# Twelve fused layers on one core: set-up steps of five stages reordered, and a small first key load

## The chip, the core and the metric

The kernel runs on one core of a Trainium2 chip. The engines are TensorE (PE, with its weight loads as PEld), VectorE (DVE), ScalarE (ACT), GpSimd (POOL) and SyncE (SP), which here only issues loads. The metric is device time in microseconds (us) of one execution, lower is better: the median of three runs of the kernel before is 1064.81 us (1062.67 to 1066.28).

## The reference

A latent `x` of 64 rows by 256 passes through four blocks of cross-attention, self-attention and feed-forward, each added to `x` after a normalisation. The context has 6272 rows of 256. Only what the change touches is shown.

```python
x = x + _L0_attn_ref(_layernorm(x), ...)      # stage 1: 16 heads, causal
x = x + _L0_ffn_ref(_layernorm(x), ...)       # stage 2: shared SiLU gate/up/down, and routed experts, top 2 of 8
x = x + _L1_xattn_ref(_layernorm(x), ctx_2048, ...)   # stage 3: queries, keys and values rounded to 8-bit steps
x = x + _L1_ffn_ref(...)                      # stage 5: LoRA experts, top 2 of 8
x = x + _L2_xattn_ref(...)                    # stage 6
#   ln_out = _ln(hidden_states, ln_w, ln_b)
#   q, k, v, qx = four fp8-rounded linear layers of ln_out; q, k, qx normalised per head of 128
#   kx, vx = split(cond @ w_kv_x); kx normalised per head
#   core = attention(q, k, v); xout = attention(qx, kx, vx)
#   out = fp8(concat(core, xout) / proj_smooth) @ wproj
x = x + _L3_attn_ref(...)                     # stage 10: short and long convolution
x = x + _L3_ffn_ref(...)                      # stage 11: 2 shared and 16 routed experts with biases b1, b2, top 4
```

## The kernel before, in words

Stages 0 to 11 follow each other, since each needs `x`. Ahead of them a sweep over the context (L1480, L1491, L1514) makes the keys and values of stages 0 and 3. Every engine has its own instruction stream, written out by hand; semaphores join them. So the order of the code within a stage is the order on the engine, and an instruction that waits holds up all that stand behind it there. Between two stages there is a serial chain: `x` gets its residual (L599), two statistics instructions (L537, L538), the variance (L548), a power on GpSimd (L562), the normalised `xn` (L542), a transpose on PE (L577), its copy on ACT (L582).

`busy(pe, n, b)` (L528) issues n products of constants that nobody reads; they only fill TensorE's time.

Weights come in pieces of up to 2048 columns (1 MB) into a ring of four slots. SP's loop (L2936) waits until `weights_used` says that a slot's old piece was used, then issues the load. The piece `x2_kx` (keys of the context in stage 6, for all eight groups of heads) is the first of stage 6 and keeps its slot through the stage; the others rotate through the other three slots.

- **Stages 0 to 2 and the rounding of the values.** Stage 3 needs the 49 tiles of values as integers. DVE makes them in nine parts of up to six tiles (`quantise`, L1706, into one of two buffers), ACT narrows each part (`narrow_values`, L1714). Part p waits until part p - 2 was narrowed. The parts are spread over stages 0, 1 and 2: in stage 1 parts 3 and 4 stand ahead of the attention and part 5 behind it; in stage 2 parts 6, 7 and 8 (the last is one tile) stand between the normalisation and the activation L892. ACT narrows them after the small tanh L925.
- **Stage 2, `f0_tensor`.** Gate and up products (L827), routed part (L868, L872), filler (6), transposes of the hidden rows (L879, L881), down product (L834), routed output (L886). DVE ranks the router's logits (L905 to L914) after the activation.
- **Stage 3, `x1_vector`.** DVE adds the bias q1 (L1934), multiplies by 0.25 (L1935), finds a step per head, rounds to `x1_q_rows` (L1940, 64x1024), PE transposes all eight pairs (L1859), DVE masks them (L1947, 128x1024), and only then the first scores (L1874) start.
- **Stages 5 and 6.** At the end of stage 5 DVE scales the low-rank rows (L1053), then waits for the whole piece `x2_kx` and centres the keys' weights of group 0 (`x2_key_weights`, L2090, L2092, L2094), and only then adds the residual (L599, L1060). PE's first products of stage 6 (L2109, keys of group 0) need those weights. Six blocks of projections follow (L2132: qx0, qx1, q0, q1, k, v), with head normalisation on DVE (`moments_of` L2354 to L2360, `normalise` L2370) and ACT (L2629), transposes on PE (`turn`, L2144), their copies on ACT (L2636), a constant product (L2150), and then the loop over groups: `variance` (L2188, L2189), `scores` (L2205), DVE's scaling (L2420).
- **Stages 10 and 11.** Stage 10 has fillers of three between its spectrum product (L1225), the inverse transform (L1234) and the output product (L1240). Stage 11 starts on PE with nine products that place the bias b1 of the expert pairs (L1327), then three fillers, then the transposes of `xn` (L577), the logits (L1331) and the experts (L1340).

## Time and profile before

| | |
|---|---|
| median of three runs | 1064.81 us (1062.67 to 1066.28) |
| profiled execution, its own time | 1061.59 us |
| its span | 1059.8 us |
| busy: PE, PEld, DVE, ACT, POOL | 994.1, 657.2, 716.2, 358.4, 156.9 us |
| share of the chain that ended last: PE, DVE, issue, DMA, ACT, POOL | 73%, 11%, 5%, 4%, 3%, 3% |
| mean granted clock of TensorE | 0.99 |

The span covers all but 1.8 us of the profiled execution. The time is 94% PE, but that is an average: from about 250 to 300 us and from 386 to 450 us, and again behind 930 us, small stages pass `x` from engine to engine, and the chain runs over DVE, ACT, POOL and loads as much as over PE.

### The profile page before, as it was taken

Reading aid. Unit: us, or ns where it says so; the run is one execution under the profiler, and the core shown is the slowest. Engines: PE = TensorE matmul, PEld = TensorE weight load, DVE = VectorE, ACT = ScalarE, POOL = GpSimd, SP = SyncE. Lnnn points to the kernel's source line nnn. Section 1 sums busy time; section 2 is a strip of 40 time slices with the busy share of each in tenths; the row PEclk is TensorE's granted clock in tenths of the full one; section 3 lists DMA queues with packets and bytes.
Section 4 is the critical chain, followed back from the end, with each engine's and each line's share of the span. In section 5 each row is a group of like instructions: output and inputs, shape, how many; then the busy total and the mean of one; then the engine's idle time right before and its main releaser. Section 6 shows DMA issues by size and latency. Waiting matters only on the chain.

```text
span 1059.8 us, 20606 instructions
## 1 busy us (share of the span) xinstructions
PE 994.1 (94%) x7822; PEld 657.2 (62%) x7846; DVE 716.2 (68%) x1909; ACT 358.4 (34%) x627; POOL 156.9 (15%) x143
## 2 busy tenths in 40 slices
PE   6999999998789988899999999999999999988898
PEld 4776677675335544365777777677777777743455
DVE  3777767768779834787676767767676767743343
ACT  2332333334428721443333333333343332301211
POOL 0000000001000010233222323222222323000000
PEclk9999999999999999998999999999999999899999
DMA  7100101002229996860000000000000000232430
GB/s 284 41 22 22 38 20 40 20 5 96 99 62 188 192 313 217 320 241 2 1 1 1 1 0 0 0 0 0 0 0 0 0 1 2 79 140 88 174 159 4
DMA packets 68729, 76.09 MB, mean 72 GB/s; under 512 B 52544, under 2 KB 59456, under 8 KB 64832
## 3 DMA queue, kind: packets, MB, share of 16 engines
q1 hardware_dynamic: 68240, 74.71, 23.1%
q8 instruction: 36, 0.59, 0.2%
q10 hardware_dynamic: 432, 0.62, 0.2%
q14 instruction: 21, 0.17, 0.0%
HBM read 62.41 MB, written 0.07 MB: 59 GB/s over the span
## 4 chain that ended last, share of the span: by engine, by line
PE 73%; DVE 11%; issue 5%; DMA 4%; ACT 3%; POOL 3%; SPq 0%; DVEq 0%; POOLq 0%; PEldq 0%
PE ps L2215 15%; PE ps L2109 13%; PE ps L1480 8%; PE ps L2205 7%; PE ps L1470 4%; PE ps L1491 4%; PE ps L1514 2%; PE ps L1526 2%; POOL x_sum L2733 2%; ACT vals L2016 2%; DMA x_keys<-vals 2%; DVE S L2420 1%; PE ps L528 1%; PE ps L1874 1%; PE ps L2817 1%
## 5 line engine op out<-in xcount | busy, mean ns | idle before, releaser
L2215 PE MATMUL ps<-vals,S 128*128 128x257 f32 x784 | 188.5, 384 | 0.7 <-ACT S L2665 0.7
L2109 PE MATMUL ps<-keysT,row_biases_sb 128*128 128x512 f32 (+1 forms) x416 | 186.3, 573 | 1.0 <-DVE row_biases_sb L2094 0.9
L2733 POOL TENSOR_TENSOR x_sum<-x_max,consts 128x4 f32<-128x4 f32 (+1 forms) x104 | 133.6, 1285 | 322.4 <-DVE x_max L2408 322.4
L2420 DVE SCALAR_TENSOR_TENSOR S<-ps,x_sum,keysT 128x128 f32<-128x128 f32 x392 | 110.9, 344 | 73.3 <-PE ps L2215 64.2
L2215 PEld LDWEIGHTS ps<-vals,S 128*128 128x128 f32 x784 | 143.3, 192 | 19.0 <-issue 1.0
L2665 ACT ACTIVATE S<-S 128x512 f32<-128x512 f32 (+1 forms) x104 | 62.7, 606 | 219.1 <-DVE S L2455 218.5
L2205 PE MATMUL ps<-x_q,x_keys 128*128 128x128 f32 x784 | 114.2, 288 | 0.0
L2109 PEld LDWEIGHTS ps<-keysT,row_biases_sb 128*128 128x128 f32 x416 | 76.6, 192 | 57.7 <-issue 52.6
L2205 PEld LDWEIGHTS ps<-x_q,x_keys 128*128 128x128 f32 x784 | 96.4, 193 | 0.0
L1480 PE MATMUL ps<-ring,S 128*128 128x512 f32 x196 | 92.2, 593 | 0.5 <-DVE ps L1621 0.5
L2597 ACT COPY x_keys<-ps 128x512 f32<-128x512 f32 (+1 forms) x104 | 57.1, 549 | 67.5 <-PE ps L2109 34.3
L1594 ACT ACTIVATE S<-ps 128x2048 f32<-128x2048 f32 (+1 forms) x25 | 46.1, 1843 | 82.3 <-PE ps L1526 76.1
L528 PE MATMUL ps<-consts 128*128 128x512 bf16 x253 | 65.7, 380 | 3.7 <-issue 0.5
L2397 DVE TENSOR_TENSOR sw_key_out<-wide 128x512 bf16<-128x512 f32 (+1 forms) x104 | 67.7, 652 | 0.7 <-ACT wide L2604 0.7
L2455 DVE TENSOR_TENSOR S<-S,xnT 128x512 f32<-128x512 f32 (+1 forms) x104 | 66.7, 654 | 0.3
L2432 DVE TENSOR_TENSOR wide<-wide,S 128x512 f32<-128x512 f32 x96 | 63.3, 659 | 0.3
L2604 ACT ACTIVATE wide<-ps 128x512 f32<-128x512 f32 (+1 forms) x104 | 60.0, 577 | 0.0
L1642 DVE TENSOR_SCALAR S<-ps,mask_sb 128x256 f32<-128x256 f32 x49 | 23.7, 484 | 52.6 <-PE ps L1480 31.1
L1470 PE MATMUL ps<-S,ring 128*128 128x256 f32 (+1 forms) x200 | 50.8, 398 | 8.9 <-DMA S<-ctxT 8.2
L1480 PEld LDWEIGHTS ps<-ring,S 128*128 128x128 f32 x196 | 35.3, 190 | 25.9 <-issue 24.7
L562 POOL TENSOR_TENSOR rstd<-var_eps,consts 64x1 f32<-64x1 f32 x13 | 7.1, 550 | 296.4 <-DVE var_eps L548 260.0
L2408 DVE TENSOR_SCALAR x_max<-ps 128x4 f32<-128x4 f32 (+1 forms) x104 | 16.5, 159 | 48.4 <-PE ps L2189 48.3
(453 smaller groups left out, 1366.1 us busy)
## 6 DMA issues: line engine op xcount, KB each, us to landing
ring<-weights SPq DMA_DIRECT2D x24, 1024.0 KB, 5.9
keysT<-ctxT SPq DMA_DIRECT2D x2, 3136.0 KB, 14.9
vals<-ctxN SPq DMA_DIRECT2D x1, 6272.0 KB, 24.3
S<-ctxT SPq DMA_DIRECT2D x12, 512.0 KB, 4.1
ring<-weights SPq DMA_DIRECT2D x6, 768.0 KB, 7.1
keysT<-weights SPq DMA_DIRECT2D x1, 1792.0 KB, 8.8
keysT<-weights SPq DMA_DIRECT2D x1, 1536.0 KB, 12.0
row_biases_sb<-row_biases SPq DMA_DIRECT2D x1, 1416.0 KB, 12.0
```

What stands on the lines that cost most here:

```text
L528: pe.matmul(ps[:, b, :], product[:, 0:128], moving, start=True, stop=True)
L1470: ins = pe.matmul(ps[:, sw_keys_bank, TWO * o:TWO * o + n * TILE], w[:, 256 * k + 128 * o:256 * k + 128 * o + 128], sw_ctxT[ph][:, k, TWO ...
L1480: ins = pe.matmul(bank(sw_vk_bank), sw_ctxT[ph][:, k, a:a + TILE], w[:, 512 + 768 * k:1024 + 768 * k], start=k == 0, stop=k == KT - 1)
L2109: ins = pe.matmul(ps[:, x2_key_bank(g, c), 0:width(c)], x2_wk[:, k, :], ctxT[:, k, span(c)], start=k == 0, stop=k == KT - 1)
L2205: ins = pe.matmul(ps[:, 3 + c % 2, 128 * s:128 * s + 128], x2_keys[:, c % 2, TILE * s:TILE * s + TILE], x2_q[:, :], start=True, stop=True)
L2215: ins = pe.matmul(bank(6, D + 1), S[:, a:a + TILE], ctx_and_ones[:, SUB * c + s, :], start=c == 0 and s == 0, stop=c == NC - 1 and s == su ...
L2397: dve.tensor_tensor(x2_low[c % 2][:, 0:width(c)], x2_dev[:, c % 2, 0:width(c)], high_half(c), ALU.subtract)\
L2420: ins = dve.scalar_tensor_tensor(S[:, a:a + TILE], ps[:, 3 + c % 2, 128 * s:128 * s + 128], x2_inv[:, c % 2, s:s + 1], x2_tile_const, ALU. ...
L2432: ins = dve.tensor_tensor(best, best, S[:, span(c)], ALU.max)
L2455: dve.tensor_tensor(chunk, chunk, spread(x2_top, 1, subs(c)), ALU.subtract).then_inc(sem("x2_shifted"), 1)
L2665: act.activation(chunk, chunk, ACT.Exp, scale=SCALE2).then_inc(sem("x2_exp"), 1)
L2733: pool.tensor_tensor(x2_inv[:, c % 2, 0:n], x2_var[:, c % 2, 0:n], C("neg_half").broadcast_to([128, n]), ALU.pow)\
```

## The change

It has seven parts. (1) Stage 1: one part of the rounding less ahead of the attention (3, then 4 behind it). (2) Stage 2: parts 5, 6 and the one-tile part (now number 7) ahead of the activation, the last six tiles (number 8) behind the router's ranking; ACT narrows in another order; the six fillers become two, and two more stand before the down product. POOL scales the bias q1 by 0.25 in this stage. (3) Stage 3: add and multiply are one instruction; rounding, transposes and mask go in two halves, the scores start after the first, and six fillers become three. (4) The 128 columns of `x2_kx` that group 0 needs are loaded by themselves, behind the last experts of stage 5, into `x2_wk`, and DVE centres them before it scales the low-rank rows. (5) The piece `x2_kx` is loaded sixth to seventh instead of first, and the pieces k, v, kx, vx are released by the end of blocks 0 to 3. (6) Stage 6: `turn(3)` before the third keys' product, the two `low_half` before the wait for the constants, ACT's `normalise(2)` one place earlier. (7) Of the nine bias products of stage 11 three each take the place of three fillers in stage 10; three remain, with four fillers behind them.

```diff
-    + [(6, "x2_kx", 2048), (6, "x2_qx0", 2048), (6, "x2_qx1", 2048), (6, "x2_q0", 2048), (6, "x2_q1", 2048), (6, "x2_k", 2048),
-       (6, "x2_v", 2048), (6, "x2_vx", 2048)]
+    + [(6, "x2_qx0", 2048), (6, "x2_qx1", 2048), (6, "x2_q0", 2048), (6, "x2_q1", 2048), (6, "x2_k", 2048),
+       (6, "x2_v", 2048), (6, "x2_kx", 2048), (6, "x2_vx", 2048)]
...
-                     10: (4, 1), 11: (3, 5)}
+                     10: (4, 1), 11: (4, 5)}
...
                 if s == 1:
-                    quantise(dve, 3, 4)
+                    quantise(dve, 3)
                 mha_vector(dve, s)
                 if s == 1:
-                    quantise(dve, 5)
+                    quantise(dve, 4)
...
-            busy(pe, 6, 6)
+            busy(pe, 2, 6)
             pe.wait_ge(sem("f0_hidden"), since("f0_hidden", 1))
...
+            busy(pe, 2, 4)
             pe.wait_ge(sem("f0_hT"), since("f0_hT", 1))
...
             norm_vector(dve, 2)
-            quantise(dve, 6, 7, 8)
+            quantise(dve, 5, 6, 7)
...
             link(dve, "dve", dve.tensor_reduce(f0_weight, f0_exp, AX, ALU.add))
+            quantise(dve, 8)
...
             norm_scalar(act, 2)
+            narrow_values(act, 5)
             act.wait_ge(sem("f0_part_psum"), 1)
             act.activation(f0_act, bank(0), ACT.Tanh, scale=0.5).then_inc(sem("f0_tanh"), 1)
+            narrow_values(act, 6)
...
-            narrow_values(act, 6, 7, 8)
...
+            narrow_values(act, 7, 8)
...
+                pool.tensor_scalar(R("q1"), R("q1"), 0.25, None, ALU.mult)
...
+            if runs(6):
+                dve.wait_ge(sem("x2_first_in"), 16)
+                x2_key_weights(dve, 0)
             dve.wait_ge(sem("f1_lows_psum"), since("f1_lows_psum", 1))
...
-            if runs(6):
-                weights_here(dve, "x2_kx")
-                x2_key_weights(dve, 0)
...
-            busy(pe, 3, 7)
+            f3_biases(pe, F3_BIASES[0])
             pe.wait_ge(sem("a3_left_ready"), since("a3_left_ready", 1))
...
-            busy(pe, 3, 7)
+            f3_biases(pe, F3_BIASES[1])
             pe.wait_ge(sem("a3_y_ready"), since("a3_y_ready", 1))
...
+        F3_BIASES = ((0, 1, 4), (2, 3, 5), (6, 7, 8))
...
+        value_parts = [(6 * i, 6 * i + 6) for i in range(7)] + [(48, NT), (42, 48)]
...
-            busy(pe, 6, 3)
+            for i in range(2):
+                pe.wait_ge(sem("x1_q_ready"), since("x1_q_ready", i + 1))
+                for j in range(4):
+                    a = 512 * i + 128 * j
+                    ins = pe.transpose(ps[:, X1_TURNED[i], j * T:(j + 1) * T], x1_q_rows[:, a:a + 128], C("ident")[0:T, 0:T])
+                ins.then_inc(sem("x1_qT_psum"), 1)
+            busy(pe, 3, 3)
...
-            link(dve, "dve", dve.tensor_tensor(x1_q, bank(0, D, T), R("q1"), ALU.add))
-            link(dve, "dve", dve.tensor_scalar(x1_q, x1_q, 0.25, None, ALU.mult))
+            link(dve, "dve", dve.scalar_tensor_tensor(x1_q, bank(0, D, T), 0.25, R("q1"), ALU.mult, ALU.add))
...
+            x1_tile_of(dve, 0)
...
+            x1_tile_of(dve, 1)
...
+        x2_behind_block = {"x2_k": 0, "x2_v": 1, "x2_kx": 2, "x2_vx": 3} if runs(5) and runs(6) else {}
...
+            turn(3)
             keys(0, 2)
-            turn(3)
...
+            low_half(0, 0)
+            low_half(0, 1)
             dve.wait_ge(sem("x2_const_ready"), since("x2_const_ready", 2))
             tile(0)
-            low_half(0, 0)
-            low_half(0, 1)
             read_var(0, 0)
+            weights_here(dve, "x2_kx")
...
             take_heads(0)
+            normalise(2)
             take_heads(1)
-            normalise(2)
...
+                if name == "f1_experts3" and runs(6):
+                    first = piece_from["x2_kx"]
+                    sp.dma_start(x2_wk, cut(io["weights"][:, first:first + KT * 1024], KT, 1024)[:, :, 0:GD]).then_inc(sem("x2_first_in"), 16)
...
-                sp.wait_ge(weights_used, release_before[n])
+                if pieces[n][1] in x2_behind_block:
+                    sp.wait_ge(sem("x2_block_psum"), x2_behind_block[pieces[n][1]] + 1)
+                else:
+                    sp.wait_ge(weights_used, n - NSLOT + 1)
                 load(n)
```

The order of the instructions at three places follows. On DVE in stage 2, from the ranking's last steps to the normalisation, first before, then now (`wide<-vals,S` is a part of the rounding, `x_sb` is `x`).

```order
L910 TENSOR_TENSOR S<-S 64x8 [waits logits_exp,dve_step]
L911 TENSOR_REDUCE S<-S 64x1 [waits dve_step]
L914 TENSOR_REDUCE S<-S 64x1 [waits dve_step]
L917 TENSOR_TENSOR x_sb<-x_sb,ps 64x256 [waits out_psum,dve_step]
L918 SCALAR_TENSOR_TENSOR x_sb<-ps,S,x_sb 64x256 [waits dve_step]
```

```order
L896 TENSOR_TENSOR S<-S 64x8 [waits logits_exp,dve_step]
L897 TENSOR_REDUCE S<-S 64x1 [waits dve_step]
L900 TENSOR_REDUCE S<-S 64x1 [waits dve_step]
L1711 TENSOR_TENSOR wide<-vals,S 128x1536 [waits values_narrowed,dve_step]
L904 TENSOR_TENSOR x_sb<-x_sb,ps 64x256 [waits out_psum]
L905 SCALAR_TENSOR_TENSOR x_sb<-ps,S,x_sb 64x256 [waits dve_step]
```

One part of the rounding moved from stage 1 to ahead of the activation, and one now stands between the ranking and the residual. On DVE at the end of stage 5, first before, then now (`x_small` holds the means of the keys' weights, `row_biases_sb` holds the centred weights):

```order
L1050 SCALAR_TENSOR_TENSOR S<-S,ps 128x128 [waits dve_step]
L1053 TENSOR_SCALAR S<-ps 64x4x16 [waits low_psum]
L2090 TENSOR_REDUCE x_small<-ring 128x2 [waits weights_in0]
L2092 TENSOR_SCALAR x_small<-x_small 128x2 [waits x2_wk_sum]
L2094 TENSOR_TENSOR row_biases_sb<-ring,x_small 128x256 [waits x2_wk_sum]
L599 TENSOR_TENSOR x_sb<-x_sb,ps 64x256 [waits out_psum]
```

```order
L1044 SCALAR_TENSOR_TENSOR S<-S,ps 128x128 [waits dve_step]
L2107 TENSOR_REDUCE x_small<-row_biases_sb 128x2 [waits x2_first_in]
L2109 TENSOR_SCALAR x_small<-x_small 128x2 [waits x2_wk_sum]
L2111 TENSOR_TENSOR row_biases_sb<-row_biases_sb,x_small 128x256 [waits x2_wk_sum]
L1050 TENSOR_SCALAR S<-ps 64x4x16 [waits low_psum]
L584 TENSOR_TENSOR x_sb<-x_sb,ps 64x256 [waits out_psum]
```

The three weight steps moved ahead of the low-rank rows and wait for the small load in place of the ring's. On PE from stage 10's spectrum product to stage 11's transposes, first before, then now (`ring,S 128x176` are the bias products, `consts 128x512` the fillers):

```order
L1225 MATMUL ps<-S,consts 65x256 [waits once_copied]
L528 MATMUL ps<-consts 128x512 x3
L1234 MATMUL ps<-consts,S 128x64 [waits once_ready]
L1240 MATMUL ps<-ring,S 64x256 [waits once_ready]
L1327 MATMUL ps<-ring,S 128x176 [waits out_psum,gates_tanh,weights_in2]
L1327 MATMUL ps<-ring,S 128x176 x8
L577 MATMUL ps<-consts,xn 128x64 [waits norm_ready]
```

```order
L1219 MATMUL ps<-S,consts 65x256 [waits once_copied]
L1324 MATMUL ps<-ring,S 128x176 [waits gates_tanh,weights_in0]
L1324 MATMUL ps<-ring,S 128x176 x2
L1228 MATMUL ps<-consts,S 128x64 [waits once_ready]
L1234 MATMUL ps<-ring,S 64x256 [waits once_ready]
L1324 MATMUL ps<-ring,S 128x176 [waits out_psum,gates_tanh,weights_in0]
L513 MATMUL ps<-consts 128x512 x4
L562 MATMUL ps<-consts,xn 128x64 [waits norm_ready]
```

Six of the nine products now stand in stage 10 (the second three, ahead of L1234, are not repeated), three where all nine stood.

## Rows read from the trace of the kernel before

**Rows 1.** Timeline, stage 1: start us, us, engine, line, what, [idle before <-releaser].
```profile
263.85 3.96 DVE L1706 TENSOR_TENSOR wide<-vals,S 128x1536 int16<-128x1536 f32 x2
...
264.65 1.94 PE L673 MATMUL ps<-ring,xnT 128*64 128x512 f32 x8 [0.45 <-ACT xnT L582]
...
267.73 0.68 DVE L727 TENSOR_TENSOR S<-ps,row_biases_sb 128x512 f32<-128x512 f32 x1
```

**Rows 2.** Timeline, stage 2.
```profile
280.67 3.43 DVE L1706 TENSOR_TENSOR wide<-vals,S 128x1536 int16<-128x1536 f32 x2
...
281.38 3.65 PE L827 MATMUL ps<-ring,xnT 128*64 128x512 f32 x16 [0.35 <-ACT xnT L582]
...
286.11 3.14 ACT L1714 CAST vals<-wide 128x1536 f16<-128x1536 int16 x3
...
287.95 0.68 DVE L892 SCALAR_TENSOR_TENSOR S<-S,ps 128x512 f32<-128x512 f32 x1
...
289.78 0.15 DVE L905 COPY S<-ps 64x8 f32<-64x8 f32 x1
...
292.56 0.15 DVE L914 TENSOR_REDUCE S<-S 64x1 f32<-64x8 f32 x1
...
293.42 0.87 DVE L917 TENSOR_TENSOR x_sb<-x_sb,ps 64x256 f32<-64x256 f32 x2 [0.70 <-PE ps L886]
```

**Rows 3.** Timeline, stage 1: a GpSimd addition beside DVE's rounding.
```profile
264.15 2.04 POOL L592 TENSOR_TENSOR x_sb<-x_sb,row_biases_sb 64x256 f32<-64x256 f32 x1
```

**Rows 4.** Timeline, stage 3 until the first scores.
```profile
300.77 0.68 DVE L1940 TENSOR_SCALAR S<-sw_key_out 64x1024 f32<-64x1024 f32 x1
...
302.15 1.47 PE L528 MATMUL ps<-consts 128*128 128x512 bf16 x6
302.33 1.22 DVE L1947 TENSOR_TENSOR x_probsT<-ps,consts 128x1024 f32<-128x1024 f32 x1 [0.38 <-PE ps L1859]
...
303.61 1.99 PE L1874 MATMUL ps<-keysT,x_probsT 32*128 32x512 f32 x12
```

**Rows 5.** Timeline, end of stage 5.
```profile
419.98 0.46 DVE L1053 TENSOR_SCALAR S<-ps 64x64 f32<-64x64 f32 x2 [3.08 <-PE ps L995]
...
421.07 0.65 PE L1019 MATMUL ps<-wide,S 128*64 128x256 f32 x2 [0.30 <-ACT S L1084]
421.41 0.42 DVE L2090 TENSOR_REDUCE x_small<-ring 128x2 f32<-128x256 f32 x1 [0.97 <-DMA ring<-weights]
...
422.52 0.41 DVE L599 TENSOR_TENSOR x_sb<-x_sb,ps 64x256 f32<-64x256 f32 x1
```

**Rows 6.** Chain of waits, set-up of stage 6: start us, us, what.
```profile
433.10 5.88 DMA ring<-weights
```

**Rows 7.** Timeline, set-up of stage 6.
```profile
428.56 5.37 PE L2132 MATMUL ps<-ring,S 128*64 128x512 f32 x24 [0.93 <-DVE S L2344]
...
449.34 0.16 DVE L2408 TENSOR_SCALAR x_max<-ps 128x4 f32<-128x4 f32 x1 [1.07 <-PE ps L2189]
```

**Rows 8.** DVE's waits, 431.28 to 449.34: total us, times, longest.
```profile
DVE S L2354 <- PE ps L2132: 1.9, 2, 1.0
...
DVE S L2370 <- POOL S L2738: 0.9, 1, 0.9
```

**Rows 9.** Timeline, stages 10 and 11.
```profile
1036.78 2.92 PE L1327 MATMUL ps<-ring,S 128*128 128x176 f32 x18 [0.30 <-PE ps L1240]
...
1038.43 0.41 DVE L542 TENSOR_SCALAR xn<-x_sb,moments,rstd 64x256 f32<-64x256 f32 x1 [0.66 <-POOL rstd L562]
...
1040.29 0.33 PE L577 MATMUL ps<-consts,xn 64*128 64x64 f32 x2
```

**Rows 10.** Timeline, keys' products at the first and second group change.
```profile
486.58 5.48 PE L2109 MATMUL ps<-keysT,row_biases_sb 128*128 128x512 f32 x8
...
546.64 3.60 PE L2109 MATMUL ps<-keysT,row_biases_sb 128*128 128x512 f32 x8
```

**Rows 11.** Stretch: us, busy us of PE, PEld, DVE, ACT, POOL; clock, DMA share, GB/s.
```profile
482.00:490.00 8.00, 6.56 (x24) 4.07 (x25) 6.98 (x21) 0.24 (x2) 3.81 (x3) 0.59 0.01 2
```

More of the change, by code:

```diff
@@ L931, in f0_scalar, with f0_pool @@
             act.activation(f0_exp, f0_exp, ACT.Exp).then_inc(sem("f0_router_exp"), 1)
-        STAGES[2] = (f0_tensor, f0_vector, f0_scalar, lambda pool: norm_pool(pool, 2))
+            narrow_values(act, 7, 8)
+        def f0_pool(pool):
+            norm_pool(pool, 2)
+            if runs(3):
+                pool.tensor_scalar(R("q1"), R("q1"), 0.25, None, ALU.mult)
+        STAGES[2] = (f0_tensor, f0_vector, f0_scalar, f0_pool)
         f1_low_weights = wide[:, :, :].rearrange("p a n -> p (a n)")[:, 0:768]
@@ L1319, in perceiver, with f3_biases @@
         f3_with = lambda m: min(m // 2 * 2 + 2, F3_PAIRS)
+        F3_BIASES = ((0, 1, 4), (2, 3, 5), (6, 7, 8))
+        def f3_biases(pe, places):
+            weights_here(pe, "f3_up0")
+            b1 = W("f3_up0")[:, 2 * F3_UP_WIDTH + KT * 16 + D:]
+            pe.wait_ge(sem("f3_selected"), since("f3_selected", 1))
+            for m in places:
+                pair = F3_ORDER[m]
+                pe.matmul(f3_bank(m), f3_select[:, 128 * pair:128 * pair + 128], b1, start=m % 2 == 0, stop=False, skip_group_check=True)
         def f3_tensor(pe):
@@ L1323, in f3_tensor @@
             w = W("f3_up0")[:, 2 * F3_UP_WIDTH:]
-            b2, b1 = w[0:NE, KT * 16:KT * 16 + D], w[:, KT * 16 + D:KT * 16 + D + FF]
-            pe.wait_ge(sem("f3_selected"), since("f3_selected", 1))
-            for m, pair in enumerate(F3_ORDER):
-                pe.matmul(f3_bank(m), f3_select[:, 128 * pair:128 * pair + 128], b1, start=m % 2 == 0, stop=False, skip_group_check=True)
+            b2 = w[0:NE, KT * 16:KT * 16 + D]
+            f3_biases(pe, F3_BIASES[2])
             norm_tensor(pe, 11)
@@ L1711, in narrow_values @@
             for part in parts:
-                a, b = 6 * part, min(6 * part + 6, NT)
+                a, b = value_parts[part]
                 act.wait_ge(sem("values_rounded"), part + 1)
@@ L1846, in x1_turn @@
             sp.dma_start_transpose(x1_probsT(j, e), x1_probs(j, e).bitcast(mybir.dt.float16)).then_inc(x1_turned(j, e)[0], 16)
+        X1_TURNED = (1, 7)
         def x1_tensor(pe):
@@ L1856, in x1_tensor @@
             busy(pe, 9, 3)
-            pe.wait_ge(sem("x1_q_ready"), since("x1_q_ready", 1))
-            for j in range(PAIRS):
-                ins = pe.transpose(ps[:, 1, j * T:(j + 1) * T], x1_q_rows[:, 128 * j:128 * j + 128], C("ident")[0:T, 0:T])
-            ins.then_inc(sem("x1_qT_psum"), 1)
-            busy(pe, 6, 3)
+            for i in range(2):
[5 more added lines that the diff above has]
+            busy(pe, 3, 3)
             def scores(j, b):
                 m = PARTS * j + b
-                if m == 0:
-                    pe.wait_ge(sem("x1_tile_ready"), since("x1_tile_ready", 1))
+                if j in (0, 4) and b == 0:
+                    pe.wait_ge(sem("x1_tile_ready"), since("x1_tile_ready", j // 4 + 1))
                 if m >= 2:
@@ L1928, in x1_tensor, with x1_tile_of @@
             out_tensor(pe, 3, attended, w[:, 512:1024], "x1")
+        def x1_tile_of(dve, i):
+            dve.wait_ge(sem("x1_qT_psum"), i + 1)
+            out = x1_queries[:, 512 * i:512 * i + 512].rearrange("p (j h t) -> p j h t", j=4, h=2)
+            dve.tensor_tensor(out, spread(cut(ps[:, X1_TURNED[i], 0:4 * T], 4, T), 2, 2), spread(spread(C("two_heads"), 1, 4), 3, T), ALU.mult)\
+               .then_inc(sem("x1_tile_ready"), 1)
         def x1_vector(dve):
@@ L1939, in x1_vector @@
             link(dve, "dve", dve.tensor_tensor(q, q, spread(x1_inv, 2, HD), ALU.mult))
-            dve.tensor_scalar(x1_q_rows.rearrange("p (j r d) -> p j r d", j=PAIRS, r=4), spread(cut(x1_q, PAIRS, 32), 2, 4), MAGIC, MAGIC,
-                              ALU.add, ALU.subtract).then_inc(sem("x1_q_ready"), 1)
+            for i in range(2):
+                pairs = slice(4 * i, 4 * i + 4)
+                dve.tensor_scalar(x1_q_rows.rearrange("p (j r d) -> p j r d", j=PAIRS, r=4)[:, pairs], spread(cut(x1_q, PAIRS, 32)[:, pairs], 2, 4),
+                                  MAGIC, MAGIC, ALU.add, ALU.subtract).then_inc(sem("x1_q_ready"), 1)
+            x1_tile_of(dve, 0)
             by_pair = cut(x1_step, PAIRS, 2)
@@ L2705, in x2_scalar @@
             take_heads(0)
+            normalise(2)
             take_heads(1)
-            normalise(2)
             copy_const(0)
+            take_heads(2)
             copy_const(1)
-            take_heads(2)
             take_values()
@@ L2935, in load @@
                 a = piece_from[name]
-                sp.dma_start(W(name), io["weights"][:, a:a + w]).then_inc(sem(f"weights_in{slot_of[n]}"), 16)
+                sp.dma_start(W(name), io["weights"][:, a:a + w]).then_inc(sem(f"weights_in{n % NSLOT}"), 16)
                 if name == "f1_lora":
```

34 lines of the change are left out of this document (8 added, 26 removed).

## Prediction

> **What bounds the kernel now.** I read the page's shares of the chain first: PE has 73% of it, yet the change leaves the sweep and the loop over groups as they are, so what matters is the chain in the short stages, where it hops from engine to engine. I then read the chain of waits from 240 to 312 us, from 386 to 500 us and behind 1016 us to find each link that belongs to a moved step, the timeline around it to see which engine was done early, and DVE's waits and the loads for the set-up of stage 6. Five links stand out. DVE rounds values while PE has finished the projections of stage 1: L673 ends at 266.59, DVE's bias add L727 starts at 267.73 [rows 1]. In stage 2 DVE is held until 287.95 though its products are there at 285.03 [rows 2]. In stage 3 eight pairs are rounded, turned and masked as wholes before a score starts [rows 4]. At the end of stage 5 the residual stands behind a 1 MB load and three weight steps [rows 5], and the set-up of stage 6 has 5.88 us of a load on the chain [rows 6]. In stage 11 `xn` is ready at 1038.84 and its transpose starts at 1040.29, because PE is still placing biases [rows 9].
>
> **The change, part by part.** All times are on the trace's clock as if everything before the part were unchanged; shifts add up, because each part is followed by a serial chain through `x`.
>
> *Stage 1.* One part of the rounding of two goes from the front. Beside GpSimd's addition one costs 3.96 / 2 = 1.98 us, so DVE is free at 265.83 and L727 follows PE's end at 266.59 plus the usual 0.07: 266.66 in place of 267.73, **1.07 saved** [rows 1]. The part behind the attention stays one part, so nothing is late there.
>
> *Stage 2.* DVE issues two parts at 1.72 each from 280.67 (3.43 for two) and a one-tile part of some 0.4, and is free at 284.6. ACT narrows part 5 from 282.4; with 1.4 to 1.5 us for a full part (3.14 for three, of which one is small) it is at 283.9, and the tanh of some 0.6 at 284.5. Both are ahead of L827's end, 285.03. So the activation L892 starts at 285.1 and not at 287.95, 2.85 earlier [rows 2]. PE's way from there to the residual was 293.42 - 287.95 = 5.47; now it ends at 290.6, or 290.9 if the two fillers that remain hold the transposes. But DVE has its own way: activation and small activation take 289.78 - 287.95 = 1.83, bringing the ranking to 286.9 to 287.05; the ranking takes 292.71 - 289.78 = 2.93, to 290.0; and now a full part of the rounding, 1.74, comes ahead of the residual, to 291.75. So the residual starts at 291.8 and not at 293.42: 1.6 saved, and 0.9 of the earlier start is lost again to that part, which nothing hides. The other two fillers stand under ACT's copy.
>
> GpSimd's scaling of q1 is new, and no row has it. Next to it stand its additions of the same 64x256: one beside DVE's rounding took 2.04 us [rows 3]. It starts as DVE starts `xn`, so its cost on the path is between nothing (two parts of rounding behind it have 0.5 us of slack before 285.1) and the 0.6 that is left of the 2.04 once the rounding instruction it stood beside is taken off (from 264.15 to its end at 263.85 + 1.72 = 265.6). I take 0.2, near the lower end, for the slack. **1.4 saved.** The Trainium skill (SBUF — State Buffer, Who interferes with whom) says that a GpSimd instruction that reads SBUF and a VectorE instruction with two SBUF inputs, or in a two-port mode, share a port pair, and the one that starts second is blocked fully. By that rule the 2.04 of rows 3 is a wait for the rounding instruction and then the work itself, and the trace agrees; for the scaling it would delay the first rounding part by up to the whole scaling, 0.6, and the sum would be 0.4 less.
>
> *Stage 3.* The separate multiply goes; a 64x256 instruction lies between a quarter of L1940's 0.68 (0.17) and L599's 0.41 [rows 4, 5]; I take 0.27 net. Then rounding in halves: half of L1940's work takes 0.40, PE's four transposes some 0.4, the half mask 0.69 (half of 1.22 and a fixed part), 1.55 from the start of the rounding to the first possible scores. But PE does the second transposes first (the second half is rounded at 0.82, turned at 1.2) and three fillers of 1.47 / 6 = 0.245: 1.95. Before, it was 303.61 - 300.77 = 2.84. Saved 0.85 to 0.9 here. DVE's step columns and second mask (0.6 and 0.7) end at about 2.9 and the first scores at 1.95 + 1.2 = 3.1, so they are hidden, with 0.2 to spare. **1.1 saved**, between 0.8 and 1.3.
>
> *End of stage 5.* DVE idles 3.08 us before L1053 [rows 5], and the three weight steps take 422.49 - 421.41 = 1.1; they fit if the small load has landed by 417. It is issued right behind the last experts (406.9), of 128 KB; even if it landed as late as a whole piece in a full queue, 5.88 us behind its issue [rows 6], it would be there at 413. The residual then follows L1019's end, 421.72, and not the weight steps: 421.74 in place of 422.52, **0.78 saved**. PE's first keys' products can start at once, and end before `xr` is there.
>
> *Set-up of stage 6.* Blocks 0 to 2 took 5.17 of the 5.37 in rows 7 without a pause; block 3 and block 4 waited for loads. Now qx0, qx1, q0, q1 are the four loads that came before, and k is issued at the end of block 0. On this part's clock, moved by 0.78: block 0 starts at 427.78, ends at 429.5; k lands 5.88 later at most, 435.4, just as turn(0) ends (DVE's normalise(0) comes at 434.8, plus 0.6). v, issued at 431.3, is there by 437.2 and needed at 438.7. So PE no longer waits and DVE becomes the bound. From 431.28 to 449.34 it spent 18.06 us, with 1.9 idle for the two late blocks, 0.9 for GpSimd behind the last of them, and 1.07 for the variances [rows 7, 8]. The first two go: 2.8. The third shrinks from 1.07 to some 0.4, since the two `low_half` come earlier but PE now has turn(3), the third keys' product of 1.7 and turn(4) between. Against that queries(1) waits some 0.35 for ACT, where normalise(2) is now ahead of take_heads(1). Step by step: DVE's own work of 14.2 us from 430.5 gives 445.05 with that wait, PE's variances end at 445.45, L2408 starts at 445.5 in place of 449.34. That is 3.85 with the 0.78, so **3.1 saved** here; 1.5 if k is as late as it can be and v with it, 3.5 at most. The load of kx (issued at 433) is needed at 445.5: hidden, by 6 us.
>
> *Stages 10 and 11.* Nine products of 2.92 us: 0.97 for three [rows 9]. In stage 10 three of them replace three fillers of 0.73; the first group may end 0.15 behind the wait of L1234, the second 0.05 behind that of L1240. In stage 11 PE is at 1036.78 + 0.97 + 4 x 0.22 = 1038.6, ahead of `xn` at 1038.84, so the transpose starts at 1038.88 and not at 1040.29: 1.4 saved, less 0.2: **1.2 saved**, between 0.8 and 1.4.
>
> Sum: 1.07 + 1.4 + 1.1 + 0.78 + 3.1 + 1.2 = 8.65, call it 8.7. The profiled execution took 1061.59, so its like would take 1052.9; the median of the runs stands 3.2 above it, at 1064.81, and I predict **1056.1** for the median.
>
> **Rivals.**
> *The loads of stage 6 stay late.* Block 4 needs k 5.9 us behind its issue, with 0 to 1 us to spare, and v is right behind it in the same queue. If both slip by the 1 to 2 us that they have to, PE waits again and the 3.1 is gone: 8.7 - 3.1 = 5.6, so 1059.2. For it: 5.88 is the only such load on the chain [rows 6]. Against: that one was issued 1.7 us behind another, this one into an empty queue.
>
> *TensorE falls to the lower clock at a touched place.* From 482 to 490 us the granted clock was 0.59, mostly at the lower of its two levels (1.2 in place of 2.4 GHz), behind a wait of PE for the weights of the next group [rows 11]; eight keys' products then took 5.48 in place of 3.60 [rows 10], 1.9 more. Fillers go in stages 2 and 3. Two such falls that were not there give 1056.1 + 3.8 = 1059.9. Against: there is less idle time around them, too. Its reverse, one fall fewer, gives 1054.2.
>
> *Slower: the inner changes of group fall too.* Between 500 and 900 us the loop changes group six times, with a wait for the weights each time, and the second change ran at the full level [rows 10]. If the changes, shifted by some 7 us, fell as the first did, it would cost 6 x 1.9 = 11.3, and the time is 1056.1 + 11.3 = 1067.4. It decides from the fifth fall on (8.7 / 1.9 = 4.6). Nothing in the order there changes, and none of six fell; a small chance.
>
> *The scaling of q1 holds up stage 2* by the whole 0.6: 1056.5, inside the range.
>
> **How the numbers follow.** The forecast, with its q1 variant, has 0.72; loads late 0.11; two falls more 0.07; one fewer 0.05; slower 0.03; the rest, 0.02, is spread. The range takes in the bounds of the terms (0.8 to 1.65 in stage 2, 0.8 to 1.3, 1.5 to 3.5, 0.8 to 1.4; together with the two small ones 5.6 to 9.7, so 1055.1 to 1059.2), the 1.5 to 2 us by which the runs shown stray from their median, and most of the two rivals above: 1053.0 to 1060.0. About what a measurement of this kernel tells from no change is 0.3%, 3.2 us: below 1061.6 counts as faster. Forecast, late loads, fewer and more falls are all faster, 0.95, less 0.02 for falls and late loads together: faster 0.93, same 0.04, slower 0.03.
>
> **What would show it.** In the profile after: the bias add of stage 1 within 0.1 of PE's end; the activation of stage 2 within 0.1 of the end of the up product, and DVE without idle time between ranking, rounding and residual; 1.9 to 2.0 from the rounding to the first scores; the residual of stage 5 right behind the last LoRA product; no wait of the projection blocks for a load, and some 15 us from the first head statistics to the first variances read; a transpose of stage 11 within 0.1 of `xn`. The forecast is wrong if the blocks still wait for loads, if the first part of the rounding in stage 2 takes 2.4 instead of 1.7, or if the granted clock is at the lower level where rows 10 and 11 do not show it.

## The result, and the profile after

The changed kernel took 1052.27 us, the median of four runs (1047.58 to 1052.5), beside 1063.74 for the kernel before in the same comparison. The ratio is 0.988, with a 95% interval of 0.984 to 0.991: it is faster, by 0.9 to 1.6%. The prediction was 1056.1, with a range of 1053.0 to 1060.0. Direction and mechanism held; the time lies 3.8 under the forecast and 0.7 under the range. The profiled execution took 1052.45 us (span 1050.6), 9.1 under that of before (1061.59, span 1059.8), where the sum had 8.7. So most of the miss is not in the sum over the stages but in the 3.2 that were added to it: the kernel before had its median 3.2 above its profiled execution, the changed one has its own 0.2 below.

All shifts below are read at one mark, the start of GpSimd's `rstd` in each stage's normalisation, which stands at every stage's beginning.

*Stage 1.* On DVE the bias add (L712) now waits for PE and follows its end at 266.93 at once, where it came 1.1 late before [rows 1]. Columns: start us, us, engine, line, operation, xcount, and in brackets the idle time before and what ended it.

```profile
264.19 1.76 DVE L1711 TENSOR_TENSOR wide<-vals,S 128x1536 int16<-128x1536 f32 x1
266.97 0.69 DVE L712 TENSOR_TENSOR S<-ps,row_biases_sb 128x512 f32<-128x512 f32 x1 [1.02 <-PE ps L658]
```

*Stage 2.* DVE after, with three parts of the rounding, the activation, and the part that now stands behind the ranking:

```profile
280.03 3.76 DVE L1711 TENSOR_TENSOR wide<-vals,S 128x1536 int16<-128x1536 f32 x3
284.52 0.69 DVE L878 SCALAR_TENSOR_TENSOR S<-S,ps 128x512 f32<-128x512 f32 x1 [0.73 <-PE ps L812]
...
289.14 0.15 DVE L900 TENSOR_REDUCE S<-S 64x1 f32<-64x8 f32 x1
289.33 1.76 DVE L1711 TENSOR_TENSOR wide<-vals,S 128x1536 int16<-128x1536 f32 x1
291.00 0.87 DVE L904 TENSOR_TENSOR x_sb<-x_sb,ps 64x256 f32<-64x256 f32 x2
```

and GpSimd's scaling of q1 with DVE's `xn` beside it:

```profile
279.44 0.89 POOL L925 TENSOR_SCALAR row_biases_sb<-row_biases_sb 64x256 f32<-64x256 f32 x1
279.48 0.51 DVE L527 TENSOR_SCALAR xn<-x_sb,moments,rstd 64x256 f32<-64x256 f32 x1 [0.66 <-POOL rstd L547]
```

The activation starts 0.13 behind the end of the products; DVE waits 0.73 for them. The rounding was not slowed: its three parts take 3.76, where two took 3.43 and the one-tile part 0.43 before. What was slowed is `xn`, 0.51 in place of 0.40, and PE's products wait for it, so the scaling cost 0.1 on the path. PE on the other side has nothing to do once its fillers are out, and idles 2.01 us ahead of stage 3's transposes:

```profile
290.04 2.32 PE L513 MATMUL ps<-consts 128*128 128x512 bf16 x10
294.37 0.33 PE L562 MATMUL ps<-consts,xn 64*128 64x64 f32 x2 [2.01 <-DVE xn L527]
295.06 1.97 PE L1861 MATMUL ps<-ring,xnT 128*64 128x256 f32 x4 [0.36 <-ACT xnT L567]
```

The last row should take 1.08 (it did before, at 297.44). The next view is that of stretches: busy time of PE, PEld, DVE, ACT and POOL, the granted clock, the DMA share and GB/s. From 294 to 300 us the clock was 0.72, so for a part of it at the lower of its two levels (1.2 GHz):

```profile
294.00:300.00 6.00, 5.22 (x21) 2.32 (x23) 2.72 (x8) 0.27 (x1) 0.72 (x1) 0.72 0.17 69
```

*Stage 3* is therefore read from a second profile of the same kernel (e1 below), with the full clock there: from the rounding of the first half to the first scores 1.95 (300.43 - 298.48), where it was 2.84 [rows 4].

```profile
298.48 0.75 DVE L1956 TENSOR_SCALAR S<-sw_key_out 64x512 f32<-64x512 f32 x2
299.45 0.69 DVE L1942 TENSOR_TENSOR x_probsT<-ps,consts 128x512 f32<-128x512 f32 x1 [0.22 <-PE ps L1868]
```

```profile
300.43 1.99 PE L1883 MATMUL ps<-keysT,x_probsT 32*128 32x512 f32 x12
```

*End of stage 5* (first profile again): the residual waits for the LoRA product alone, and the key weights' three steps are done at 413.8, inside the wait before L1050 (L1053 in [rows 5]).

```profile
413.38 0.42 DVE L2111 TENSOR_TENSOR row_biases_sb<-row_biases_sb,x_small 128x256 f32<-128x256 f32 x1
415.98 0.46 DVE L1050 TENSOR_SCALAR S<-ps 64x64 f32<-64x64 f32 x2 [2.18 <-PE ps L989]
417.75 0.41 DVE L584 TENSOR_TENSOR x_sb<-x_sb,ps 64x256 f32<-64x256 f32 x1 [1.31 <-PE ps L1013]
```

*Set-up of stage 6.* The chain (start us, us, what) holds no load any more [rows 6]. It runs through PE without a pause from the first block to the last turn:

```profile
423.77 7.09 PE ps L2149 x32
430.86 0.65 PE ps L2161 x4
431.51 1.87 PE ps L2149 x8
...
438.14 0.59 PE ps L2161 x4
438.73 1.72 PE ps L2126 x4
440.45 0.44 PE ps L2161 x4
...
441.10 0.17 DVE x_max L2425
```

DVE's waits up to 445 us (total us, times, longest) have neither the blocks nor GpSimd's L2738 [rows 8]; L2425 at 441.10 does not wait, and the wait left for this line is that for the next variances, at 444.16, inside the loop:

```profile
DVE S L2357 <- ACT S L2629: 0.5, 1, 0.5
DVE x_max L2425 <- PE ps L2206: 0.5, 1, 0.5
DVE row_biases_sb L2400 <- ACT S L2654: 0.2, 1, 0.2
```

*Stage 11.* Three biases are left, and the transpose follows `xn` (L527) at once [rows 9]:

```profile
1029.06 1.13 PE L1324 MATMUL ps<-ring,S 128*128 128x176 f32 x6 [0.33 <-PE ps L1234]
...
1031.14 0.34 PE L562 MATMUL ps<-consts,xn 64*128 64x64 f32 x2
```

### The profile page after: what moved, and what is told of

Same layout as the page of the kernel before. It is cut to its first block, busy times and chain, and to the rows that moved or that the text cites. A ratio compares the mean times of both kernels' runs of the same rounds, so it can differ in the third digit from the quotient of the medians.

```text
span 1050.6 us, 20593 instructions
## 1 busy us (share of the span) xinstructions
PE 991.0 (94%) x7812; PEld 655.7 (62%) x7836; DVE 715.7 (68%) x1910; ACT 358.4 (34%) x627; POOL 157.4 (15%) x144
## 4 chain that ended last, share of the span: by engine, by line
PE 73%; DVE 11%; issue 6%; ACT 3%; POOL 3%; DMA 3%; SPq 0%; DVEq 0%; POOLq 0%
PE ps L2232 15%; PE ps L2126 12%; PE ps L1483 8%; PE ps L2222 7%; PE ps L1473 4%; PE ps L1494 4%; PE ps L1517 2%; PE ps L1529 2%; POOL x_sum L2751 2%; ACT vals L2031 2%; DVE S L2437 1%; PE ps L513 1%; DMA x_keys<-vals 1%; PE ps L1883 1%; PE ps L2835 1%
## 5 line engine op out<-in xcount | busy, mean ns | idle before, releaser
L2425 DVE TENSOR_SCALAR x_max<-ps 128x4 f32<-128x4 f32 (+1 forms) x104 | 16.5, 159 | 48.0 <-PE ps L2206 47.8
```

## The experiments

### The parts apart (e1 to e4)

e1 is the changed kernel again. e2 applies the changes of stages 1 to 3 alone to the kernel before, e3 those around the second cross-attention (stages 5 and 6) alone, e4 the biases of the last feed-forward alone. The edits are abridged here and below:

```diff
 e2  -quantise(dve, 3, 4) / (5) / (6, 7, 8)      +quantise(dve, 3) / (4) / (5, 6, 7) ... (8); x1 in halves
 e3  -(6, "x2_kx", 2048) first                   +x2_kx behind x2_v, x2_first load, SP waits on blocks, order of stage 6
 e4  -busy(pe, 3, 7) twice in stage 10           +f3_biases(pe, F3_BIASES[0]), [1]
```

> The changed kernel once more, beside the kernel before. Theory A (the terms of the sum are right and only the base was wrong: the before runs' median of 1064.81 was set against terms read from a profiled execution at 1061.59): the profiled time lies near 1052.5, and the difference of the medians over more runs comes to 9 to 10 us, not 11.5. Theory B (the change brings 2 to 3 us that no term of mine holds): the difference stays at 11 to 12 us and the profile shows a stage that is shorter than worked out.

> The kernel before with the changes of stages 1, 2 and 3 alone (where the value groups are quantised, the filler counts of stage 2, the halves of the first cross-attention's query). Theory A: stage 1 gives 1.1, stage 2 1.7, stage 3 between 0.4 (with TensorE's clock falling at its head, as in the changed kernel's profile) and 1.1 (without), so 3.2 to 3.9 us less than before, and if the fall at stage 3's head belongs to this part, the one before stage 5 (408 to 411 us) is gone here too. Rival: the 3.4 us fall at stage 5 is set by what stage 5 holds; then it stays here and a second one comes on top, and the gain is near 2.5 us.

> The kernel before with the changes around the second cross-attention alone (its first key load, the order of the weight pieces and their waits, and the order of the set-up). Theory A: 0.8 at the end of stage 5 and 3.1 in stage 6, 3.9 us less than before, with the clock fall at 408 us in place. Rival (the fall in stage 5 goes with the key weights' move): 1.2 us more, 5.1.

> The kernel before with the nine bias matmuls of the last feed-forward in the gaps of stage 10 alone. Theory A: stage 10 loses 0.1, stage 11 gains 1.4, so 1.3 us less than before. Rival (the six filler groups that they replace are missed, and TensorE's clock falls at the head of stage 11): nothing or a loss of up to 1 us.

Measured: e1 1051.66 (ratio 0.988, 0.986 to 0.991), e2 1059.5 (0.996, 0.994 to 0.998), e3 1057.98 (0.995, 0.993 to 0.998), e4 1060.83 (0.999, 0.997 to 1.001), beside 1063.13 for the kernel before over 24 runs. The three parts give 3.6 + 5.2 + 2.3 = 11.1, the whole 11.5. Each of these differences is known to about 2 us, so they show no interaction, but could hide one of that size. The profile of e1 took 1051.62. Theory B of e1 found support in one number, the difference of the medians, which stayed at 11.5 and did not come down to 9 to 10; its other half, a stage shorter than worked out, holds for stage 3 alone (table below). e2's profile had a clock fall at 297 us and the one at 406 as well, so the fall before stage 5 does not belong to what stages 1 to 3 do. e3's median came 5.2 lower, which is the number of its rival, but not for the rival's reason: its profile still has the fall in stage 5, which took 19.22 in place of 19.99. e4's stage 11 was 1.4 shorter and its stage 10 0.08 longer, as worked out, though its interval reaches no change.

### Profiles of the same two kernels again (e5, e6, e13 to e16)

Nothing is edited; what is asked is how two executions of one kernel differ.

> The kernel before, unchanged, with a second profile. Theory A (its ordinary runs stand above its first profiled one because TensorE's clock falls in more, or in dearer, places): a profiled run at 1063 or more shows falls that the first (408, 483, 903, 988 us) did not have, at a granted clock at or under 0.990, and each stretch without a fall is as long as before within 0.2 us. Rival B: the granted clock is the same and a stretch that no fall touches (the sweep up to 262 us, which moves data) is 1 to 3 us longer.

> The same kernel for a third profile, for how many of the falls repeat from execution to execution. Theory A: the places vary, each fall outside the group loop costs 0.9 to 1.7 us, and the sum over the places gives the difference of the spans within 0.5 us. Rival B: the falls sit in the same four places and the spans differ for another reason.

> The kernel before, a fourth profile. Theory A (its ordinary runs carry falls in stage 2, at the head of stage 5, in the set-up of stage 6 and in stages 9 and 10, and first loads that land later than in the first profile): a span of 1060 to 1063 whose difference from the first profile's 1059.8 is the sum, within 0.3 us, of falls that are there in one and not in the other (0.9 to 2 us each by place) and of the stretch up to the first norm behind the sweep. Rival B: stretches without a fall differ too.

> The changed kernel, a third profile. Theory A: no fall in stage 2 and one at the head of stage 3 in about every second profile; stage 1 16.9 - 1.09, stage 2 14.41, stage 3 91.4 without a fall and 92.5 with one, stage 5 18.0 without a fall; span between 1045.8 and 1051.5. Rival B: the stages' lengths without falls scatter by more than 0.2 us.

> The kernel before, a fifth profile, as the fourth. What is counted over all of them: in how many a fall stands in stage 2 (2 of 3 so far), in stage 5 (3 of 3), in the first part of stage 6 (3 of 3), in stage 9 or 10 (1 of 3).

> The changed kernel, a fourth profile, as the third. What is counted: in how many a fall stands in stage 2 or at the head of stage 3 (1 of 2 so far), in stage 5 (0 of 2), in the first part of stage 6 (2 of 2), in stage 9 or 10 (2 of 2). Theory A: fewer in all than in the kernel before by one to two.

e5's runs had a median of 1062.79 (ratio 1.001, 0.999 to 1.004). A fall is a stretch in which the granted clock is at the lower of its two levels. The table has the stretches between two marks, in us, in the order first profile, e5, e6, e13, e15 of the kernel before and first profile, e1, e14, e16 of the changed one (* marks a stretch in which the clock record has a fall that the others lack; the last column is the gain where neither has one):

```
stage       before                                  changed                        gain
sweep       249.58  251.86  251.15  249.58  250.31  249.57  250.28  249.64  249.57
1            16.87   16.86   16.88   16.86   16.86   15.78   15.77   15.77   15.78   1.09
2            16.07   17.76*  17.42*  17.75*  16.06   14.41   14.42   14.40   14.40   1.66
3            92.91   92.93   92.99   92.89   92.87   92.54*  91.42   92.50*  92.52*  1.49
5            19.99*  19.95*  20.23*  18.97   18.91   18.01   17.99   17.90   19.21*  1.0
6           515.65  516.65* 515.65  515.58  517.31* 512.57  512.52  512.63  512.62   3.05
8b and 9     63.95*  62.33   62.34   62.33   63.97*  63.97*  63.97*  63.96*  63.96*
10           13.64   13.64   13.64   13.63   13.64   13.72   13.72   13.72   13.72  -0.08
11 to end    21.95   21.93   21.96   21.94   21.96   20.50   20.48   20.48   20.54   1.45
profile    1061.59 1064.30 1063.05 1060.87 1062.79 1052.45 1051.62 1052.31 1053.86
```

(Stages 4, 7 and the first norm of 8 were equal within 0.03 in all. 8b is stage 8 from its second mark. In stage 6, falls at about 485 and 905 us before, 476 and 895 after, are in all nine profiles and not marked, nor are those in the last 10 us.)

Three things are to be seen. A stretch without an extra fall repeats within 0.12 us from execution to execution, so one profile does give a stage's length. A fall costs 1.4 to 1.7 in stage 2, 1.1 at stage 3's head, 1.0 to 1.3 in stage 5 and 1.6 in stage 9, where it is there, and whether it is there changes from execution to execution. And the sweep, which nothing touches, takes between 249.6 and 251.9. Of its two rows for 13 to 30 us the first is of the first profile (sweep 249.58), the second of e5 (251.86). The longer sweep goes with a lower DMA share (0.52 against 0.63) and less work on DVE (11.26 us busy against 12.78) there, so its loads or what waits for them seem to be behind; what sets that is not shown:

```profile
13.00:30.00 17.00, 17.00 (x178) 11.66 (x177) 12.78 (x39) 4.49 (x5) 0.56 (x1) 1.00 0.63 245
```

```profile
13.00:30.00 17.00, 17.00 (x164) 10.98 (x166) 11.26 (x35) 3.30 (x4) 0.19 (x1) 1.00 0.52 210
```

Theory A held for the stages and rival B for the sweep: both make an ordinary run longer than the first profile. Theory A's last count did not hold. By place there are ten extra falls in five profiles of the kernel before (three in stage 2, three in stage 5, two in stage 6, two in stage 9) and eight in four of the changed one (three at stage 3's head, one in stage 5, four in stage 9): two for each execution of either. Nor is the fall at the first change of group a constant: it is in all nine of these profiles, but those of e4, and of e7, e8, e9 and e11 below, lack it. In those of them with the changed kernel's stage 6 (e7, e9, e11) the stage takes 510.44 to 510.55 in place of 512.52 to 512.63, which makes this the dearest of the falls that come and go. The clock over 470 to 500 us, of the changed kernel and of e11:

```profile
470.00:500.00 30.00, 27.29 (x155) 18.46 (x154) 21.53 (x63) 9.23 (x19) 9.28 (x7) 0.89 0.00 1
```

```profile
470.00:500.00 30.00, 26.00 (x168) 17.68 (x167) 22.08 (x66) 9.21 (x19) 9.28 (x7) 1.00 0.01 2
```

### The late group, and the order without which the loads do (e7, e8)

e7 takes the rounding part that costs 0.9 ahead of the residual out of stage 2:

```diff
 f0_vector:  -quantise(dve, 8)
 x1_vector:   norm_vector(dve, 3)
             +quantise(dve, 8)
 f0_scalar:  -narrow_values(act, 7, 8)
             +narrow_values(act, 7)
 x1_scalar:   norm_scalar(act, 3)
             +narrow_values(act, 8)
```

> The changed kernel with its last six-tile part of the rounding taken out of stage 2, where 0.9 us of it stood between the ranking and the residual, and put behind xn in stage 3, where DVE waits for the query product (ACT narrows it there). Theory (the 0.9 is on the path, and the wait in stage 3 of 1.5 to 2 us covers it): stage 2 is 0.9 us shorter, stage 3 longer by 0 to 0.3, the whole 0.6 to 0.9 us less than the changed kernel. Rival (PE's products set the residual of stage 2 anyway, or the rounding of 1.7 us does not fit in stage 3's wait): no gain, or a loss of 0.3.

It took 1048.08 (ratio 0.987, 0.984 to 0.989; six runs, 1046.14 to 1049.26), against 1051.66 and 1052.27 for the changed kernel. Stage 2 was 13.41 in place of 14.41, 1.0 shorter; stage 3 91.59 in place of 91.42. That 0.17 is not the part's: the first scores come 6.64 behind the mark, where it was 6.71 in e1, and in e9 and e12, with the same edit, the stage takes 91.24 and 91.38. The part fits into DVE's wait for the query product almost exactly, the next instruction follows it without one:

```profile
292.88 1.76 DVE L1710 TENSOR_TENSOR wide<-vals,S 128x1536 int16<-128x1536 f32 x1
294.71 0.42 DVE L1949 SCALAR_TENSOR_TENSOR sw_key_out<-ps,row_biases_sb 64x256 f32<-64x256 f32 x1
```

So the theory is right for 1.0; the rest of the 3.6 to 4.2 between the medians is falls: this profile has one in stage 5 and none at 295, 475 or 980, and lies at 1047.55. That the edit itself brings fewer falls is not shown: e9 and e12, which hold it too, have a median of 1049.8 over twelve runs. PE's gap at stage 3's head is 1.01 here and not 2.01:

```profile
292.90 0.33 PE L562 MATMUL ps<-consts,xn 64*128 64x64 f32 x2 [1.01 <-DVE xn L527]
```

e8 has e3's loads, with the set-up of stage 6 in its old order:

```diff
 e3 to e8:  keys(0, 2) ahead of turn(3) again; low_half(0, 0), low_half(0, 1) behind tile(0) again;
            take_heads(1), normalise(2) and take_heads(2) in their old places
```

> The kernel before with the loads around the second cross-attention changed (small first key load, the order of the pieces, SP's waits on the blocks), but with its set-up in the old order on PE, DVE and ACT. Theory: the loads carry most of the 3.1 us of stage 6 (2.8 for the two late blocks and GpSimd behind them), the order only the rest, the wait for the variances; so stage 5 gives 0.8 and stage 6 2.0 to 2.8. Rival (with the loads early, DVE is the bound, and without the new order it waits 1.1 us for PE's variances and 0.9 for GpSimd as before): stage 6 gives 1.2 or less.

1058.16 (0.996, 0.994 to 0.998), beside 1057.98 for e3. From the mark of stage 6 to the first variances read it took 22.18 (446.29 - 424.11), where it was 25.03 before and 21.55 with the order as well: the loads carry 2.85 and the order 0.63 of 3.48, of which 3.05 is left at the end of the stage. The rival, that DVE and its old waits are the bound, is out; only the wait for the variances stands as before (1.07 then, 1.06 here), and the order is what takes it away:

```profile
446.29 0.16 DVE L2395 TENSOR_SCALAR x_max<-ps 128x4 f32<-128x4 f32 x1 [1.06 <-PE ps L2176]
```

### Idle time of PE and the clock (e9 to e12)

e10 fills stage 2's gap of 1.71 us in the kernel before (0.20 is left); e11 the one of 2.01 in the changed kernel (0.50 is left); e12 the one of 1.01 in e7 (0.36 is left); e9 puts stage 5's first expert products into a gap of 0.85 in e7:

```diff
 e10  -busy(pe, 6, 6)            +busy(pe, 13, 6)
 e11  -BUSY_NORM 3: (10, 3)      +3: (17, 3)
 e12  -BUSY_NORM 3: (10, 3)      +3: (13, 3)
 e9   -pe.wait_ge(f1_low_ready) ahead of up(0)
      +in up(0), behind its eight matmuls on xnT
```

> The kernel of the late group, with the first eight expert products of stage 5 issued ahead of PE's wait for the LoRA inputs, which fills 0.85 us of PE's idle time there. Without a fall DVE's ranking sets stage 5 (18.0 us in both profiles of the changed kernel), so nothing is gained on that path. Theory A (idle time of PE at that place brings the clock fall at 403 to 412 us): the profile has no fall there, stage 5 takes 18.0 to 18.1, and the runs' mean clock rises to 0.995 or more. Rival B (the fall has its cause in something else, such as where the last fall was): a fall between 398 and 412 still shows, and stage 5 takes 18.9 to 19.3 with it.

> The kernel before, with 13 filler matmuls in place of 6 in stage 2, so that PE's idle time of 1.71 us ahead of the activation's transposes is filled; the fillers (0.23 us each) end within 0.1 us of the activation. Theory A (two of the three profiles of the kernel before have a fall in stage 2 at 291 to 293 us, 1.35 to 1.7 us long, because PE idled there): the fall is gone from this place, the mean clock of the runs rises by about 0.001 from 0.990 and the median is 1 to 1.5 us under that of the kernel before. Rival B (the changed kernel has fewer falls for another reason, as the mean clock of 0.990 of the kernel with stages 1 to 3 alone suggests): clock and median stay within 0.5 us and 0.0005 of the kernel before, and a fall may come elsewhere.

> The changed kernel with 17 filler matmuls in place of 10 ahead of stage 3's transposes, where its rounding part ahead of the residual leaves PE idle for 2.01 us. Theory A (PE's long idle time brings the clock fall that one of two profiles shows at 295 us, 1.1 us long): no fall between 286 and 300, stage 3 takes 91.4 and not 92.5, the runs' mean clock rises from 0.9925 by about 0.001 and their median falls by 0.5 to 1 us from 1051.9. Rival B (the falls do not follow this gap): a fall at 295 or 296 shows, and clock and median stay.

> The kernel of the late group, with 13 fillers in place of 10 in the gap of 1.01 us that it leaves at the same place. Theory A (a gap of 1 us already risks a fall): the mean clock goes above 0.9945 and the median to 1047.5. Rival B (1 us of idle time brings no fall, and the fillers may hold the transposes by up to 0.2 us): the median stays at 1048 to 1048.3.

e10 took 1060.92 (0.998, 0.996 to 1.000), its runs' mean clock was 0.9921 (89 runs of the kernel before: 0.9899). Three rows of stage 2 stand for it, of the first profile of before, of e5 and of e10. The stage has the same 16.07 with PE busy for 12.65 or 14.38; the fall (clock 0.90) makes it 17.76:

```profile
279.65:295.72 16.07, 12.65 (x73) 6.02 (x71) 10.51 (x28) 4.97 (x9) 0.55 (x2) 1.00 0.51 174
```

```profile
281.34:299.10 17.76, 14.55 (x74) 6.80 (x71) 10.51 (x28) 4.97 (x9) 0.55 (x2) 0.90 0.47 161
```

```profile
281.91:297.98 16.07, 14.38 (x81) 6.71 (x78) 10.49 (x28) 4.97 (x9) 0.55 (x2) 1.00 0.49 174
```

What the fall does in e5 is 3.46 us for the down product that takes 1.95 at the full level, the next large product behind the gap:

```profile
291.09 0.66 PE L879 MATMUL ps<-consts,S 128*128 128x128 f32 x4 [1.71 <-DVE S L893]
...
292.63 3.46 PE L834 MATMUL ps<-ring,S 128*64 128x256 f32 x16 [0.68 <-ACT S L928]
```

e11 has no fall at stage 3's head and 91.38 for the stage, but 1051.77 for the median of four runs and a mean clock of 0.9922: the same as the changed kernel's. e12 came to 1051.34 (0.987, 0.985 to 0.990), with runs from 1046.6 to 1054.4, no better than e7. e9 had no fall in its profile but those at 889 us and in the last microseconds (1046.1, the shortest taken; stage 5 17.90), but 1049.51 over six runs and a mean clock of 0.9935, under e7's 0.9945. So at these two places a fall goes with idle time of PE: with a gap of 2.01 at stage 3's head four of five profiles have it there (the changed kernel's and e2's), with 1.01 or a filled one none of four (e7, e9, e11, e12), and with the 0.98 of the kernel before none of its five; in stage 2 it is four of eight with the gap of 1.71 and none of ten without. The gap alone does not decide: at the first change of group PE idles the same 1.47 ahead of the fall in the changed kernel (L2205 at 475.10) and in e7, e9 and e11, which have none there. How many falls a run has was lower in one trial of filling a gap (e10) and not in the three others. Theory A of e10 is supported; those of e9 and e11 hold in the profile (no fall at the place, the stage at its short length) and not in the runs' clock; that of e12 is not supported.

## Why the prediction was wrong, and where it was right

*The step that failed is the base*: "the median of the runs stands 3.2 above it, at 1064.81, and I predict 1056.1 for the median." It treats 3.2 as something that a profile lacks and every run has, before the change and after it. It is the difference between one favourable execution (the short sweep of 249.58, no fall in stage 2) and the middle of three runs that lay high. Over 89 runs the kernel before has a median of 1063.24, 1.65 above its first profile; the changed kernel over 12 has 1052.16, 0.3 under its own. Set against the profiled execution alone, the sum's 1052.9 would have been 0.6 from the result, but in part by luck, since the medians of all runs are 11.1 apart and the sum had 8.7. From the median of 89 runs the sum gives 1054.6, inside the range and still 2.3 too high. The range was built around the wrong centre, and its lower end of 1053.0 fell just above the time; its lower bounds also add to 5.75, not to 5.6.

*The sum was a little short*: 9.7 by the table's last column, where 8.65 was forecast.
- Stage 1: 1.09 for 1.07.
- Stage 2: 1.66 for 1.4. The scaling of q1 took 0.89, not 0.6; of the 0.2 set for it 0.1 was lost, by a longer `xn` and not by a held-up rounding part as put. The 0.9 that the part behind the ranking costs is real: e7 got 1.0 back by moving it.
- Stage 3: 1.49 for 1.1. The stretch from rounding to scores is the 1.95 worked out. The multiply gave 0.29, so that 1.18 were there at the first scores. The next six pairs keep it; another 0.34 came at the seventh of the eight, which took 9.06 before and 8.72 after. No step had that, and its cause is open.
- Stage 5: 1.0 for 0.78. Where no fall holds the experts up, the large load that the key weights waited for was later still against them: in e13 the residual came 1.10 behind the end of L1019, in the first profile 0.80.
- Set-up of stage 6: 3.05 for 3.1, but not by the step as put. DVE was said to become the bound; it is PE, whose blocks, turns and keys' product of 1.72 now run on without a pause. By e8 the loads carry 2.85 and the order 0.63 at the first variances.
- Stages 10 and 11: 1.45 - 0.08 for 1.4 - 0.2.

*The rivals.* The loads did not stay late, the scaling cost 0.1 and not 0.6, no inner change of group fell that had not. More or fewer falls at touched places is what happened in part: stage 2 lost its fall and stage 3's head got one, at 1.1 where 1.9 was set, and in the pair of profiles that one was paid back in stage 5. The pair thus shows 9.1 and hides the trade. One sign of being wrong came true with it: the clock was at its lower level where rows 10 and 11 do not show it, at 294 to 299 us. The sign was no good one, since the first profile has falls at 408 and 988 us as well, outside those rows. And the fall at 483 us was read as behind a wait for the next group's weights; the clock is low from about 483.4, behind PE's 1.47 of waiting for DVE's `sw_key_out` (L2397), and 3 us ahead of the keys' products at 486.58.

*What stays open.* The means of the five and four profiles are 1062.52 and 1052.56, 9.96 apart: 9.7 of stages, 0.7 of a shorter sweep, less what lies ahead of the first mark, and about equal falls. The medians of all runs are 11.1 apart. About 1 us of the gain is thus in no profile. That the changed kernel's runs have fewer falls is likely (mean clock 0.9919 over 12 runs, 0.9899 over 89), but by place it was not seen, and the fall at the first change of group, which some of its runs may lack as e11 does, was in all four of its profiles. Nor is it settled whether its sweep is shorter or only was so in four profiles.

## What to carry to other kernels

Set a sum of terms against the execution that they were read in, and ask of the difference to the median which stretches make it up before it is carried over: here it was a sweep that ended later by up to 2.3 us and a clock fall, not a constant. When a step is moved off the path, look at the engine that now idles longer; a gap of 2 us that is harmless by the chain can be where TensorE's clock falls. And a rounding or set-up part is best put where its engine already waits: the same 1.76 us cost 1.0 ahead of a residual and nothing inside the wait behind the next norm.

## What the runs showed of the hardware that was not expected

A stretch without a fall repeats within 0.12 us over executions and chips in the nine profiles of the two kernels (the same stage 3 differs by 0.35 between e7 and e9), while whole runs of one kernel spread over 14 us (1059.1 to 1073.0); the spread goes with the granted clock, 1059.8 on average at 0.994, 1063.6 at 0.990 and 1071.8 at 0.982. A fall behind a gap took the next product of 1.95 us to 3.46. A 64x256 `xn` on DVE took 0.51 in place of 0.40 beside a GpSimd instruction that had started 0.04 ahead of it. With the same instructions the sweep ended up to 2.3 us later in some executions, with a lower DMA share in its first 30 us.
